# A top-2 mixture of experts in units of two tiles, with weights stationary in the first product and rows added to the output by indirect DMA

## The chip, the cores and the metric

The kernel runs as one program on one core of one Trainium2 chip. The metric is the device time of one execution in microseconds. Three runs of the kernel before took 2163.88, 2171.52 and 2172.83 us; the median is 2171.52 us. The engines are TensorE (PE, its weight loads PEld), VectorE (DVE), ScalarE (ACT), GpSimd (POOL) and SyncE (SP); PEq, SPq and so on are their instruction queues.

## The reference

A batch of 4 images of 256 channels by 32 x 32 positions goes through a Mamba block, a dense product, a channel attention and at last a mixture of experts. Only the last is touched. It sees 4096 tokens of 256 floats, 8 experts and the best 2 experts for each token:

```python
B, S, D = (8, 1024, 256)
E, K, H = (8, 2, 1024)
...
gate_logits = x_flat @ gate_w.T
topk_vals, topk_idx = jax.lax.top_k(gate_logits, K)
topk_w = jax.nn.softmax(topk_vals, axis=-1)
comb = comb.at[jnp.arange(T)[:, None], topk_idx].add(topk_w)
for e in range(E):
    h = jax.nn.gelu(x_flat @ w1[e].T + b1[e], approximate=False)
    y = h @ w2[e].T + b2[e]
    out = out + comb[:, e:e + 1] * y
...
t = t + _L1_ffn_ref(_ln_t(t), L1_ffn_gate_w, ...)
```

All products are in 32-bit floats.

## The kernel before

`build_front` computes everything ahead of the experts. It leaves the normalised tokens in DRAM (`xm_rows`, one row of 1 KB a token), the residual in `x3_dram`, the gate logits in SBUF, and all expert weights in SBUF (`W1`, `W2` inside `experts_sb`). `build_moe` is the stage in question.

**Routing.** VectorE finds the two best experts of each token, TensorE counts tokens by expert with two products, and VectorE turns counts into places. Each expert's list is padded to whole tiles of 128 rows, so that there are always `NT` = 71 tiles. Each step of `step(...)` waits for the one before. Eight rounds of one-hot matrices (L1780 to L1790), multiplied on TensorE, then give for every tile the token of each of its rows (`TAB`, the row to fetch) and the row of `y_rows` to write (`ROW`). `TE` holds the expert of every tile.

**The expert loop, one tile at a time.** Every engine walks the 71 tiles in the order in which its program is written; semaphores tie them together. For a tile t:

- GpSimd gathers 128 rows of `xm_rows` into `XG` by indirect DMA (`gather`, L1562 to L1568, four buffers). It copies the column of indices into `IX` first. It then scatters finished rows: `scatter`, L1570 to L1577, writes `YS` to `y_rows` by indirect DMA. In the loop the gather of tile t stands ahead of the scatter of tile t - 6 (L1592 to L1596).
- TensorE turns the two halves of the rows (`turn_rows`, L1622), multiplies by the expert's first weights (`up`, L1630: the rows stationary, 512 hidden columns moving, 4 products), turns the 8 blocks of the hidden rows (`turn_hidden`, L1639), and multiplies by the second weights (`down`, L1647: 8 products with 256 columns moving). A product of 32-bit floats is two matmul records in the profile, a turn is one. Its `step` (L1662) runs `turn_hidden(t - 1)`, `turn_rows(t + 1)`, `up(t)`, `down(t - 1)`.
- VectorE copies the turned rows (`rows_turned`, L1808) and the hidden rows (`hidden`, L1812) from PSUM, and adds the second bias (`result`, L1816). ScalarE applies the gelu with the first bias from the turned hidden rows (L1693).

**The last part.** When all scatters have landed, SP loads both rows of every token from `y_rows` (L1553) and the last quarter of the residual (L1554). ScalarE and VectorE scale the two rows by their gates and add them to the residual (L1708, L1851, L1855), and SP writes `out` (L1557).

All products of `build_moe` are issued by the helper `mm`, so they all have line 1606 in the profile; their operands tell them apart: `XGT_sb` is `up`, `hgt_sb` with `experts_sb` is `down`, line 1643 is `turn_hidden`, line 1627 is `turn_rows`.

## Time and profile before

| | |
|---|---|
| median of three runs | 2171.52 us |
| profiled execution, its own time | 2172.07 us |
| span of its trace | 2170.1 us |
| mean granted TensorE clock | 0.909 |
| TensorE busy, whole span | 1652.3 us |
| VectorE busy | 1435.5 us |
| GpSimd busy | 1146.9 us |
| ScalarE busy | 868.3 us |
| first `up` of the expert loop starts | 1546.27 us |
| last `down` ends | 2123.78 us |

The shares of the whole span mix stages with different limits. Up to about 1490 us the program is `build_front`, which the change leaves alone apart from where the residual is stored. From there to 1539 us it is the routing, to 2124 us the expert loop, and to the end the last part. A granted clock of 1.00 is 2.4 GHz, 0.50 is 1.2 GHz. Starts are counted from the start of the span.

### The profile page before, as it was taken

The page shows a single profiled execution, that of the slowest core. Times are in us where ns is not written, and L with a number is a line of the kernel's source. Part 1 is how long each engine was busy: PE and PEld are TensorE (multiplying, and loading weights), DVE is VectorE, ACT ScalarE, POOL GpSimd, SP SyncE. Part 2 cuts the span into 40 slices and gives each one's busy share as a digit, 9 for nine tenths or more (in the row PEclk, how much of TensorE's full clock was granted, in tenths as well). Part 3 has the DMA queues.
Part 4 walks back from the last instruction along what each step waited for, and adds up shares of the span by engine and source line. Part 5 has one row for each costly group of instructions (what it writes and reads, how often), then busy time and mean ns, then how long its engine had stood idle before and what let it go on. Part 6 is the DMA issues. An engine that isn't in the chain of part 4 may idle for free. (4 is left out here: it accounts for less than half of the span.)

```text
span 2170.1 us, 22230 instructions
## 1 busy us (share of the span) xinstructions
PE 1652.3 (76%) x5692; PEld 922.6 (43%) x5693; DVE 1435.5 (66%) x1492; ACT 868.3 (40%) x1535; POOL 1146.9 (53%) x708
## 2 busy tenths in 40 slices
PE   5357777677778766777778777664699999999990
PEld 2122234342224443222445222344377667666770
DVE  3989996679997858999577999845422222222224
ACT  6535425464432664543456443221122332233223
POOL 2699872569894438988155989500222332233210
PEclk9789998889999888999877999976799999999995
DMA  3075530055561016654004656443011100110107
GB/s 113 6 250 215 202 127 22 5 177 205 194 223 58 5 30 246 208 198 156 23 5 159 212 194 205 185 191 118 24 32 34 34 31 31 34 34 31 31 23 256
DMA packets 76307, 245.72 MB, mean 113 GB/s; under 512 B 10364, under 2 KB 24197, under 8 KB 71366
## 3 DMA queue, kind: packets, MB, share of 16 engines
q1 hardware_dynamic: 69414, 226.17, 29.9%
q0 software_dynamic: 6816, 18.62, 2.7%
q8 instruction: 37, 0.61, 0.1%
q14 instruction: 40, 0.33, 0.0%
HBM read 220.76 MB, written 23.99 MB: 113 GB/s over the span
## 5 line engine op out<-in xcount | busy, mean ns | idle before, releaser
L368 PE MATMUL psum<-HC_sb,ident_sb 128*128 128x512 f32 x1024 | 492.0, 604 | 59.5 <-DVE HC_sb L1320 57.9
L368 PE MATMUL psum<-experts_sb 64*128 64x512 f32 (+4 forms) x962 | 348.3, 572 | 235.9 <-DVE HC_sb L1320 148.1
L913 ACT ACTIVATE psum<-experts_sb 128x1024 f32<-128x1024 f32 x256 | 285.2, 1117 | 476.0 <-DVE experts_sb L1310 387.9
L1310 DVE TENSOR_TENSOR_SCAN experts_sb<-psum,DBX_sb 128x1024 f32<-128x1024 f32 x172 | 390.0, 2277 | 29.6 <-POOL DBX_sb L1017 28.6
L368 PEld LDWEIGHTS psum<-experts_sb 64*128 64x128 f32 (+4 forms) x962 | 116.6, 168 | 495.4 <-DVE HC_sb L1320 242.9
L368 PEld LDWEIGHTS psum<-HC_sb,ident_sb 128*128 128x128 f32 x1024 | 191.1, 192 | 272.7 <-issue 131.5
L1693 ACT ACTIVATE hgt_sb<-psum_moe,b_sb 128x128 f32<-128x128 f32 x568 | 154.3, 382 | 359.3 <-PE psum_moe L1643 359.1
L1606 PE MATMUL psum_moe<-experts_sb,hgt_sb 128*128 x1136 | 259.4, 382 | 4.1 <-ACT hgt_sb L1693 2.6
L1576 POOL DMA_INDIRECT y_rows<-YS_sb,iy_sb x71 | 70.8, 998 | 356.6 <-PE psum_moe L1627 221.7
L1606 PE MATMUL psum_moe<-experts_sb,XGT_sb 128*128 x568 | 257.0, 595 | 0.3 <-issue 0.3
L1606 PEld LDWEIGHTS psum_moe<-experts_sb,hgt_sb 128*128 128x128 f32 x1136 | 216.3, 191 | 66.8 <-issue 40.6
L1320 DVE TENSOR_TENSOR HC_sb<-psum,experts_sb 128x1024 f32<-128x1024 f32 x192 | 230.7, 1201 | 0.1
L1814 DVE COPY hg_sb<-psum_moe 128x1024 f32<-128x1024 f32 x71 | 87.0, 1225 | 216.5 <-PE psum_moe L1606 216.5
L1017 POOL TENSOR_TENSOR DBX_sb<-DA_sb,experts_sb 128x1024 f32<-128x1024 f32 x88 | 206.1, 2352 | 11.4 <-DVE experts_sb L1310 9.6
L1310 DVE TENSOR_TENSOR_SCAN experts_sb<-psum,SQ_sb 128x1024 f32<-128x1024 f32 x84 | 191.2, 2277 | 0.0
L1025 POOL TENSOR_TENSOR HC_sb<-X_XT_sb,experts_sb 128x1024 f32<-128x1024 f32 x64 | 150.5, 2351 | 76.1 <-PE psum L368 76.0
L1822 DVE TENSOR_TENSOR YS_sb<-psum_moe,b_sb 128x256 f32<-128x256 f32 x71 | 30.2, 425 | 180.8 <-PE psum_moe L1606 180.8
L1606 PEld LDWEIGHTS psum_moe<-experts_sb,XGT_sb 128*128 128x128 f32 x568 | 102.9, 191 | 103.4 <-issue 103.4
L962 POOL TENSOR_TENSOR experts_sb<-experts_sb 128x1024 f32<-128x1024 f32 x16 | 40.4, 2525 | 130.5 <-DVE experts_sb L1095 130.5
L1017 POOL TENSOR_TENSOR DBX_sb<-SQ_sb,experts_sb 128x1024 f32<-128x1024 f32 x44 | 103.5, 2352 | 0.0
L1567 POOL DMA_INDIRECT XG_sb<-xm_rows,ix_sb x71 | 70.4, 991 | 58.1 <-POOL ix_sb L1564 58.1
L950 POOL TENSOR_TENSOR experts_sb<-experts_sb 64x1024 f32<-64x1024 f32 x16 | 37.9, 2369 | 111.1 <-ACT experts_sb L752 109.7
(248 smaller groups left out, 2179.2 us busy)
## 6 DMA issues: line engine op xcount, KB each, us to landing
DA_sb<-b_rows SPq DMA_DIRECT2D x128, 512.0 KB, 4.8
experts_sb<-b_rows SPq DMA_DIRECT2D x64, 512.0 KB, 3.6
SQ_sb<-b_rows SPq DMA_DIRECT2D x64, 512.0 KB, 4.7
X_XT_sb<-c_rows SPq DMA_DIRECT2D x64, 512.0 KB, 5.5
experts_sb<-w1T SPq DMA_DIRECT2D x8, 1024.0 KB, 19.3
experts_sb<-w2T SPq DMA_DIRECT2D x8, 1024.0 KB, 21.3
experts_sb<-y_rows SPq DMA_DIRECT2D x8, 1024.0 KB, 11.8
X_sb<-x_tok SPq DMA_DIRECT2D x5, 1024.0 KB, 6.9
```

Of the source, the lines that this page charges most:

```text
L368: return nc.tensor.matmul(o, lhsT, rhs, start=start, stop=stop, **k)
L913: nc.scalar.activation(decays[i % 2], DT[:, c, :], ACT.Exp, scale=a_neg[:, s:s + 1]).then_inc(da_ready, 1)
L962: nc.gpsimd.tensor_tensor(DT[:, c, :], DTX[:, c, :], log_tile(c), ALU.add).then_inc(dt_done, 1)
L1017: nc.gpsimd.tensor_tensor(DRIVE[i % STATE_SLOTS], B_REP[k], DTX[:, c, :], ALU.mult).then_inc(drive_ready, 1)
L1025: nc.gpsimd.tensor_tensor(HC[:, i % 2, :], C_REP[q % 2], STATE[i % STATE_SLOTS], ALU.mult).then_inc(pool_read, 1)
L1310: v.tensor_tensor_scan(STATE[i % STATE_SLOTS], decays[i % 2], DRIVE[i % STATE_SLOTS], 0.0, ALU.mult, ALU.add).then_inc(h_ready, 1)
L1320: v.tensor_tensor(halves(HC[:, i % 2, :]), crep, halves(STATE[i % STATE_SLOTS]), ALU.mult).then_inc(dve_read, 1)
L1567: pool.indirect_dma_start(XG[:, k, :], None, xm_rows, bass.IndirectOffsetOnAxis(ap=IX[:, k:k + 1], axis=0)).then_inc(xg_ready[k], 16)
L1576: pool.indirect_dma_start(y_rows, bass.IndirectOffsetOnAxis(ap=IY[:, k:k + 1], axis=0), YS[:, k, :], None).then_inc(y_stored[k], 16)
L1606: return nc.tensor.matmul(o, lhsT, rhs, start=start, stop=stop, **k)
L1693: m = nc.scalar.activation(HGT[:, j, :], psum[:, 2 + j // 4, (j % 4) * P:(j % 4 + 1) * P], ACT.Gelu, bias=b1[:, bass.ds(e, 1), j])
L1814: v.tensor_copy(HG[:, :].rearrange("p (h n) -> p h n", h=NH), psum[:, 0:2, :]).then_inc(hg_done, 1)
```

## The change

- Tiles are taken in units. The first 32 units hold two tiles of one expert, the last 7 hold one tile, 39 units for the same 71 tiles. An expert's even tiles go to the paired units, an odd one to a single unit; the routing computes places for both.
- In `up` the first weights are stationary, in blocks of 128 x 128, and the turned rows of the unit move (256 columns, 128 for a single unit): 16 products a unit. The hidden rows come out turned already. `turn_hidden` and the copy `hidden` are gone; ScalarE reads the product itself. For this, VectorE copies the expert's first weights from `experts_sb` to one of two buffers `W1S` for every unit (`copy_weights`, 128 x 2048 floats).
- Each result row is scaled by its gate in `result` by a second VectorE instruction. The gates are turned on TensorE, written to DRAM (`gate_rows`), and gathered for every tile by an indirect DMA of 128 single floats (`gather_gate`).
- `build_front` stores the residual into `out` itself. The rows are added there by an indirect DMA that adds (`scatter_add`). Each of these waits until the one before has landed (semaphore `added`). `y_rows`, `x3_dram` and the whole last part are gone.
- GpSimd's indirect DMAs read their indices from the tables, without the copies to `IX` and `IY`, and its program is written out without a loop. TensorE's `step` is `turn_rows(u + 1)`, `up(u)`, `down(u - 1)`.

The diff, cut to its core; removed functions stand above:

```diff
-RING = 4
-TAIL = RING * (NT // RING - 1) + 1
-Y_ROWS = 3 * TOK + NT * P
-R_DIF, R_CHOSEN, R_ALL = 14, 15, 42
+PAIRS = 32
+UNITS = PAIRS + NT - 2 * PAIRS
+OUT_ROWS = TOK + 2 * P
+R_DIF, R_CHOSEN, R_ALL = 14, 15, 56
...
-                sp.dma_start(x3_dram[b], X2[:, :, :]).then_inc(stored, 16)
+                sp.dma_start(out[0:TOK, :].rearrange("(b n p) c -> b p n c", n=NB, p=P)[b], X2[:, :, :]).then_inc(stored, 16)
...
+        HGT = sb("hgt", [P, 2, HB, 2 * P])
+        W1S = sb("w1s", [P, 2, CT, HID])
+        XG = sb("XG", [P, 4, C])
+        XGT = sb("XGT", [P, 2, CT, 2 * P])
+        YS = sb("YS", [P, 4, C])
...
+            sp.wait_ge(gates_copied, 1)
+            sp.dma_start(gate_rows.rearrange("(a p) o -> a (p o)", p=P), P21T[:, :]).then_inc(gates_stored, 16)
+            sp.wait_ge(gates_stored, 16)
+            sp.wait_ge(added, NT * 16)
...
+            def gather(tile):
+                k = slots(tile)
+                if tile >= 4:
+                    pool.wait_ge(t1_ready, (tile // 2 if tile < 2 * PAIRS else tile - PAIRS) - 1)
+                pool.indirect_dma_start(XG[:, k, :], None, xm_rows,
+                                        bass.IndirectOffsetOnAxis(ap=TAB[:, tile:tile + 1], axis=0)).then_inc(xg_ready[k], 16)
+
+            def gather_gate(tile):
+                pool.indirect_dma_start(PS[:, tile:tile + 1], None, gate_rows,
+                                        bass.IndirectOffsetOnAxis(ap=GIX[:, tile:tile + 1], axis=0)).then_inc(
+                                            gate_there[slots(tile)], 16)
+
+            def scatter_add(tile):
+                pool.wait_ge(y_done, tile + 1)
+                if tile:
+                    pool.wait_ge(added, tile * 16)
+                pool.indirect_dma_start(out, bass.IndirectOffsetOnAxis(ap=SCAT[:, tile:tile + 1], axis=0),
+                                        YS[:, tile % 4, :], None, compute_op=ALU.add).then_inc(added, 16)
 
             pool.wait_ge(tab_done, 1)
+            for tile in range(4):
+                gather(tile)
+            pool.wait_ge(tab_done, 2)
+            pool.wait_ge(gates_stored, 16)
+            for tile in range(4):
+                gather_gate(tile)
+            for u in range(UNITS):
+                if u + 2 < UNITS:
+                    for j in range(width(u + 2)):
+                        gather(first_tile(u + 2) + j)
+                    for j in range(width(u + 2)):
+                        gather_gate(first_tile(u + 2) + j)
+                for j in range(width(u)):
+                    scatter_add(first_tile(u) + j)
...
+            def turn_rows(u, k, ready):
+                for j in range(width(u)):
+                    pe.wait_ge(xg_ready[2 * k + j], ready)
+                if not isinstance(u, int) or u >= 2:
+                    pe.wait_ge(xgt_done, u - 1)
+                for j in range(width(u)):
+                    for c in range(CT):
+                        m = nc.tensor.transpose(psum[:, 6 + k, c * 2 * P + j * P:c * 2 * P + (j + 1) * P],
+                                                XG[:, 2 * k + j, c * P:(c + 1) * P], ident[:, :])
                 m.then_inc(t1_ready, 1)
 
+            def up(u, k):
+                w = width(u) * P
+                pe.wait_ge(w1_copied, u + 1)
+                pe.wait_ge(xgt_done, u + 1)
                 for h in range(NH):
+                    if not isinstance(u, int) or u:
+                        pe.wait_ge(gelu_done, u * 2 + (h - 1))
+                    for q in range(4):
+                        for c in range(CT):
+                            m = mm(psum[:, 2 * h + q // 2, (q % 2) * 2 * P:(q % 2) * 2 * P + w],
+                                   W1S[:, k, c, (4 * h + q) * P:(4 * h + q + 1) * P], XGT[:, k, c, 0:w],
+                                   c == 0, c == CT - 1)
+                    m.then_inc(m1_ready, 1)
...
+            def down(u, k):
+                e = pe.value_load(TE[0:1, bass.ds(u, 1)], min_val=0, max_val=E - 1)
+                if not isinstance(u, int) or u:
+                    pe.wait_ge(y_biased, first_tile(u))
+                pe.wait_ge(gelu_done, u * 2 + 2)
+                for j in range(width(u)):
+                    for q in range(HB):
+                        m = mm(psum[:, 4 + j, 0:C], HGT[:, k, q, j * P:(j + 1) * P], W2[:, bass.ds(e, 1), q, :],
+                               q == 0, q == HB - 1)
+                    m.then_inc(m2_ready, 1)
...
+            def step(u, k, ready):
+                turn_rows(u + 1, (k + 1) % 2, ready)
+                up(u, k)
+                down(u - 1, (k + 1) % 2)
...
+            def gelu(u, k):
+                w = width(u) * P
+                e = act.value_load(TE[0:1, bass.ds(u, 1)], min_val=0, max_val=E - 1)
+                if not isinstance(u, int) or u >= 2:
+                    act.wait_ge(m2_ready, first_tile(u - 1) if isinstance(u, int) else u * 2 - 2)
+                for h in range(NH):
+                    act.wait_ge(m1_ready, u * 2 + (h + 1))
...
+                step(v.tensor_tensor(EQ[:, :, :], POS[:, :, :], by_expert(PAIRF[:, :]), ALU.is_lt))
+                step(v.tensor_tensor(EQ[:, :, :], EQ[:, :, :], by_expert(DELTA[:, :]), ALU.mult))
+                step(v.tensor_tensor(POS[:, :, :], POS[:, :, :], by_expert(SHIFT[:, :]), ALU.add))
+                step(v.tensor_tensor(POS[:, :, :], POS[:, :, :], EQ[:, :, :], ALU.add))
...
+            def copy_weights(u, k):
+                e = dve.value_load(TE[0:1, bass.ds(u, 1)], min_val=0, max_val=E - 1)
+                if not isinstance(u, int) or u >= 2:
+                    dve.wait_ge(m1_ready, u * 2 - 2)
+                v.tensor_copy(W1S[:, k, :, :].unsqueeze(1), W1[:, bass.ds(e, 1), :, :]).then_inc(w1_copied, 1)
+
+            def result(u, j, there, free):
...
+                v.tensor_tensor(ys.unsqueeze(1), psum[:, 4 + j, 0:C].unsqueeze(1), b2[:, bass.ds(e, 1), :],
+                                ALU.add).then_inc(y_biased, 1)
+                dve.wait_ge(gate_there[there[1]], there[2])
+                dve.wait_ge(y_biased, tile + 1)
+                v.tensor_scalar(ys, ys, PS[:, bass.ds(tile, 1)], None, ALU.mult).then_inc(y_done, 1)
```

**GpSimd, before**, one turn of the loop over tiles. L1567 is the gather of tile t, L1576 the scatter of tile t - 6; `t1_ready` is raised by `turn_rows`, `y_copied` by `result`:

```order
L1564 ISA [waits t1_ready]
L1564 COPY ix_sb<-tab_sb 128x1
L1565 REGISTER_ALU
L1567 DMA XG_sb<-xm_rows,ix_sb 128x256 [waits ix_ready]
L1595 ISA
L1572 ISA [waits y_stored0]
L1572 COPY iy_sb<-row_sb 128x1
L1573 REGISTER_ALU
L1576 DMA y_rows<-YS_sb,iy_sb 21376x256 [waits iy_ready,y_copied]
```

**GpSimd, changed**, from the start of the stage through the passes u = 0 and u = 1 of its loop over units. L1561 is a gather of rows, L1565 one of gates, L1573 an adding scatter; `y_done` is raised by the scaling in `result`:

```order
L1561 DMA XG_sb<-xm_rows,tab_sb 128x256 [waits tab_done]
L1561 DMA XG_sb<-xm_rows,tab_sb 128x256 x3
L1565 DMA ps_sb<-gate_rows,gix_sb 128x1 [waits gates_stored,tab_done]
L1565 DMA ps_sb<-gate_rows,gix_sb 128x1 x3
L1561 DMA XG_sb<-xm_rows,tab_sb 128x256 [waits t1_ready] x2
L1565 DMA ps_sb<-gate_rows,gix_sb 128x1 x2
L1573 DMA out<-YS_sb,scat_sb 4352x256 [waits y_done]
L1573 DMA out<-YS_sb,scat_sb 4352x256 [waits added,y_done]
L1561 DMA XG_sb<-xm_rows,tab_sb 128x256 [waits t1_ready] x2
L1565 DMA ps_sb<-gate_rows,gix_sb 128x1 x2
L1573 DMA out<-YS_sb,scat_sb 4352x256 [waits added,y_done] x2
```

The gathers of pass u are those of unit u + 2, and they stand behind the scatters of unit u - 1; before, the gather of a tile stood behind the scatter of the tile seven earlier.

**TensorE, before**, one step of the loop over tiles, the eight `down` products shown by the first:

```order
L1643 MATMUL psum_moe<-m_ident_sb,hg_sb 128x128 x8
L1627 MATMUL psum_moe<-m_ident_sb,XG_sb 128x128 x2
L1606 MATMUL psum_moe<-experts_sb,XGT_sb 128x512
L1648 TENSOR_LOAD te_sb
L1606 MATMUL psum_moe<-experts_sb,hgt_sb 128x256
```

**TensorE, changed**, one step of the loop over units:

```order
L1622 MATMUL psum_moe<-m_ident_sb,XG_sb 128x128 [waits xgt_done,xg_ready3,xg_ready2]
L1622 MATMUL psum_moe<-m_ident_sb,XG_sb 128x128 x3
L1632 ISA [waits xgt_done,w1_copied]
L1595 MATMUL psum_moe<-XGT_sb,w1s_sb 128x256 [waits gelu_done]
L1595 MATMUL psum_moe<-XGT_sb,w1s_sb 128x256 x7
L1595 MATMUL psum_moe<-XGT_sb,w1s_sb 128x256 [waits gelu_done]
L1595 MATMUL psum_moe<-XGT_sb,w1s_sb 128x256 x7
L1641 TENSOR_LOAD te_sb
L1644 REGISTER_ALU [waits y_biased]
```

The eight turns of hidden rows are gone; the turns of the next unit's rows, with their wait for both gathers, are now the first thing in a step, ahead of the products of the present unit.

## Rows read from the trace of the kernel before

**Rows 1.** The page, 40 slices of 54.3 us: engines and granted clock.
```profile
PE   5357777677778766777778777664699999999990
PEclk9789998889999888999877999976799999999995
```

**Rows 2.** Busy time by stretch (TensorE, weights, VectorE, ScalarE, GpSimd, clock, DMA).
```profile
1600.00:1700.00 100.00, 99.60 (x427) 69.51 (x427) 25.74 (x38) 29.84 (x103) 29.50 (x49) 1.00 0.10 32
2100.00:2172.00 72.00, 21.21 (x83) 14.96 (x81) 30.51 (x70) 22.05 (x56) 4.52 (x7) 0.66 0.56 197
```

**Rows 3.** Chain of waits: start, us, engine, tile, line, count.
```profile
1729.69 0.87 PE psum_moe L1643 x8
1730.78 6.89 PE psum_moe L1606 x24
...
1746.75 3.43 PE psum_moe L1606 x8
...
2125.14 2.43 DMA y_rows<-YS_sb,iy_sb
```

**Rows 4.** Timeline, entry of the expert stage.
```profile
1503.45 0.17 DVE L1753 TENSOR_SCALAR padi_sb<-padi_sb 128x8 uint32<-128x8 uint32 x1
...
1504.28 0.42 DVE L1757 TENSOR_TENSOR incl_sb<-incl_sb,tot_sb 128x256 f32<-128x256 f32 x1
1504.73 0.42 DVE L1758 TENSOR_TENSOR incl_sb<-incl_sb,start_sb 128x256 f32<-128x256 f32 x1
...
1538.84 0.20 DVE L1800 TENSOR_SCALAR tab_sb<-row_sb 128x71 uint32<-128x71 uint32 x1
...
1540.26 1.16 POOL L1567 DMA_INDIRECT XG_sb<-xm_rows,ix_sb  x1 [0.97 <-POOL ix_sb L1564]
...
1542.46 0.98 POOL L1567 DMA_INDIRECT XG_sb<-xm_rows,ix_sb  x1 [0.84 <-POOL ix_sb L1564]
...
1545.29 0.69 PE L1627 MATMUL psum_moe<-m_ident_sb,XG_sb 128*128 128x128 f32 x2 [1.31 <-DMA XG_sb<-xm_rows,ix_sb]
...
1546.27 5.04 PE L1606 MATMUL psum_moe<-experts_sb,XGT_sb 128*128 x8 [0.28 <-issue]
```

**Rows 5.** Timeline, last tile and what follows it.
```profile
2118.38 5.40 PE L1606 MATMUL psum_moe<-experts_sb,hgt_sb 128*128 x16 [2.57 <-ACT hgt_sb L1693]
2123.93 0.42 DVE L1822 TENSOR_TENSOR YS_sb<-psum_moe,b_sb 128x256 f32<-128x256 f32 x1 [8.42 <-PE psum_moe L1606]
2125.14 0.99 POOL L1576 DMA_INDIRECT y_rows<-YS_sb,iy_sb  x1 [7.66 <-DVE YS_sb L1822]
```

**Rows 6.** Timeline of two tiles: start, length, engine, line, operation, [idle <-releaser].
```profile
1710.12 3.21 PEld L1606 LDWEIGHTS psum_moe<-experts_sb,hgt_sb 128*128 128x128 f32 x15 [0.24 <-issue]
...
1713.57 1.04 PE L1643 MATMUL psum_moe<-m_ident_sb,hg_sb 128*128 128x128 f32 x8
1713.89 0.43 DVE L1822 TENSOR_TENSOR YS_sb<-psum_moe,b_sb 128x256 f32<-128x256 f32 x1 [2.35 <-PE psum_moe L1606]
...
1714.66 3.60 PE L1606 MATMUL psum_moe<-experts_sb,XGT_sb 128*128 x8
```

**Rows 7.** DMA issues: queue, operation, count, KB each, median us to landing.
```profile
xm_rows<-X_XT_sb SPq DMA_DIRECT2D x4, 1024.0 KB, 4.7
```

**Rows 8.** Gathers of line 1567: who waited (us, times), and time to landing.
```profile
  PE psum_moe L1627: 6.4, 2
...
DMA to landing us min/median/max: 2.6/2.8/3.7
```

**Rows 9.** Busy time by stretch around the last down product.
```profile
2115.00:2118.30 3.30, 0.81 (x8) 0.57 (x6) 0.42 (x1) 2.17 (x8) 1.18 (x2) 1.00 0.11 40
2118.30:2120.30 2.00, 1.92 (x6) 1.61 (x7) 0.00 (x0) 0.00 (x0) 0.00 (x0) 0.68 0.00 0
2120.30:2122.30 2.00, 2.00 (x6) 1.55 (x6) 0.00 (x0) 0.00 (x0) 0.00 (x0) 0.50 0.00 0
2122.30:2124.00 1.70, 1.48 (x7) 0.97 (x5) 0.07 (x1) 0.00 (x0) 0.00 (x0) 0.96 0.00 0
```

More of the change, by code:

```diff
@@ L1468, in lay_out, with build_moe @@
     return a
-def build_moe(nc, t, x3_dram, xm_rows, y_rows, logits, routing, experts, out):
+def build_moe(nc, t, xm_rows, gate_rows, logits, routing, experts, out):
     with ExitStack() as ctx:
@@ new lines, in build_moe @@
+        tab_step = sem("tab_step"); tab_done = sem("tab_done")
+        gates_turned = sem("gates_turned"); gates_copied = sem("gates_copied"); gates_stored = sem("gates_stored")
+        xg_ready = [sem(f"xg_ready{k}") for k in range(4)]; gate_there = [sem(f"gate_there{k}") for k in range(4)]
+        t1_ready = sem("t1_ready"); xgt_done = sem("xgt_done"); w1_copied = sem("w1_copied"); m1_ready = sem("m1_ready"); gelu_done = sem("gelu_done")
+        m2_ready = sem("m2_ready"); y_biased = sem("y_biased"); y_done = sem("y_done"); added = sem("added")
@@ L1540, in build_moe, with width, first_tile, slots @@
         C_ALL = 16 * len(consts)
+        def width(u):
+            return 2 if not isinstance(u, int) or u < PAIRS else 1
+        def first_tile(u):
+            return 2 * u if not isinstance(u, int) or u < PAIRS else u + PAIRS
+        def slots(tile):
+            return tile % 4 if tile < 2 * PAIRS else 2 * ((tile - PAIRS) % 2)
+        def uses(tile):
+            return sum(slots(i) == slots(tile) for i in range(tile + 1))
         @block.sync
@@ L1620, in _ @@
                 i.then_inc(onehot_used, 1)
[L1622 to L1627 removed]
+                if g == 0:
+                    pe.wait_ge(route, R_ALL)
+                    pe.wait_ge(c_loaded, C_ALL)
+                    nc.tensor.transpose(psum[0:2 * NG_, 3, 0:P], P21[:, :, :].rearrange("p j n -> p (j n)"),
+                                        ident[:, :]).then_inc(gates_turned, 1)
@@ L1824, in _ @@
             dve.wait_ge(c_loaded, C_ALL)
+            copy_weights(0, 0)
             rows_turned(0, 0)
+            copy_weights(1, 1)
             rows_turned(1, 1)
-            hidden(0)
-            for k in range(RING):
-                rows_turned(k + 2, k % 2)
-                hidden(k + 1)
-                result(k, k % 2, 16 if k >= 2 else None)
-            with dve.Fori(1, NT // RING - 1) as i:
-                for k in range(RING):
-                    rows_turned(i * RING + (k + 2), k % 2)
-                    hidden(i * RING + (k + 1))
-                    result(i * RING + k, k % 2, i * 32 + (k // 2) * 16)
@@ new lines, in _ @@
+            copy_weights(2, 0)
+            for j in range(2):
+                result(0, j, (j, j, 16), None)
+            rows_turned(3, 1)
+            copy_weights(3, 1)
+            for j in range(2):
+                result(1, j, (2 + j, 2 + j, 16), None)
+            with dve.Fori(1, PAIRS // 2 - 1) as i:
+                for k in range(2):
+                    rows_turned(i * 2 + (k + 2), k)
+                    copy_weights(i * 2 + (k + 2), k)
+                    for j in range(2):
+                        result(i * 2 + k, j, (2 * k + j, 2 * k + j, i * 16 + 16), i * 64 + (32 * k + 16 * j - 48))
@@ L1858 @@
+            for u in range(PAIRS - 2, UNITS):
+                if u + 2 < UNITS:
+                    rows_turned(u + 2, u % 2)
+                    copy_weights(u + 2, u % 2)
+                for j in range(width(u)):
+                    tile = first_tile(u) + j
+                    result(u, j, (tile % 4, slots(tile), 16 * uses(tile)), 16 * (tile - 3))
 def kernel(**inputs):
```

297 lines of the change are left out of this document (98 added, 199 removed).

## The prediction

> **What bounds the kernel now.** I read the 40 slices first: TensorE's row turns from sevens into nines, and its clock into tens, three quarters of the way [rows 1]. That is the expert loop. The busy times by stretch then give it as 99.60 of 100 us of TensorE at a granted clock of 1.00, with VectorE, ScalarE and GpSimd under a third, and the end of the program as something else, 21 of 72 us [rows 2]. The chain of waits shows the loop's beat: 6.89 us of products, 0.87 us of turned hidden rows (L1643), again and again, with no other engine in it [rows 3]. From 1729.69 to 1730.78 and on, a tile takes 0.87 + 0.22 (row turns) + 6.89 = 7.98 us; 71 tiles are 566.6 us of the 577.5 us from the first `up` at 1546.27 [rows 4] to the last `down`'s end at 2118.38 + 5.40 = 2123.78 [rows 5]. So in the loop everything that leaves TensorE is won, and only while TensorE is still never kept waiting. Behind the loop stand 2170.1 - 2123.78 = 46.3 us in which TensorE has nothing to do.
>
> My sum is made against the profiled execution's own 2172.07 us, 0.55 us above the median of the runs, so it needs no correction.
>
> **What is taken off TensorE.** `turn_hidden` is 8 turns a tile, 0.87 us in the chain [rows 3]: 7.98 becomes 7.11 us a tile. `up` in its new form is 16 products, 32 records, of 256 columns with new weights each. That form stands in the trace as `down`: 15 weight loads go by in 3.21 us, 0.214 us each [rows 6]. So a unit of two takes 32 x 0.214 = 6.85 us, against 2 x 3.43 = 6.86 us now [rows 3]: nothing won or lost. In the 7 single units 32 records with 128 columns go at the beat of the turns, 0.87 / 8 = 0.109 us: 3.49 against 3.43 us, 0.4 us in all. If those weight loads didn't overlap, they would cost up to 0.19 us each, 0.08 us x 32 x 7 = 18 us more; I take none, since the turns in the trace load weights at the same beat.
> From first `up` to last `down` TensorE then needs 71 x 7.11 - 0.88 (two units' row turns, now ahead of it) + 0.4 = 504.3 us, and 1.6 us for a start at the low clock, as now (5.04 against 3.43 us, [rows 3, 4]): 505.9 against 577.5 us, -71.6 us. In this are 62 us of turns; the other 10 are waits of the first and the last tile that the new order doesn't have, such as 2.57 us for the last gelu [rows 5].
>
> **The end.** From the last `down` on: 0.16 us to the bias, 0.42 us for it [rows 5], 0.04 us to the next instruction, 0.30 us for the scaling (between 0.2 and 0.43, what a 128 x 256 VectorE instruction takes), 0.79 us until GpSimd starts (2123.93 + 0.42 to 2125.14), about 3.1 us until the added rows have landed (the plain scatter took 2.43 us, [rows 3]), 0.2 us to the end: 5.0 against 46.3 us, -41.3 us.
>
> **The routing** gets 11 steps more of 8 elements at 0.17 + 0.04 = 0.21 us [rows 4], two more of 256 elements net (two fall away, four come) at 0.46 us, one more of 0.2 us and the copy of the turned gates, 0.3 us: 2.3 + 0.9 + 0.5 = +3.7 us. All of it is in VectorE's chain, on which the first gather waits. Then `up(0)` waits for four gathers where it waited for two. The first is issued 0.8 us after the table (now 0.97 behind a copy), four take 1.16 + 0.99 x 2 + gaps of 0.4 between starts, and the last lands 2.83 us after its start (1542.46 to 1545.29, [rows 4]). That is 8.0 + 0.9 us after the table against 1546.27 - 1539.04 = 7.2 us now, +1.6 us. Nothing waits for the gates: they are first used when `down(0)` is over. The residual stored in rows of 1 KB has the shape of the `xm_rows` store, which lands in 4.7 us on a queue that nobody waits for then [rows 7]: 0.
>
> So far 2172.07 - 71.6 - 41.3 + 5.3 = **2064.5 us**, if TensorE never waits inside the loop.
>
> **The wait that comes in.** It does wait. GpSimd's pass u issues the gathers of unit u + 2, then two of gates, then the scatters of unit u, and the pass before ended with the scatters of unit u - 1. These need `down(u - 1)`, the last thing in TensorE's step u. The first thing in step u + 1 is `turn_rows(u + 2)`, which needs those gathers. They are issued only when the step is over, and behind `turn_rows(u + 2)` stand `up(u + 1)` and `down(u)`, whose inputs have long been there. Before, six tiles lay between: TensorE waited for a gather twice [rows 8], both times at the entry. The length of the wait, from the last `down` of a step to the first turn of the next:
> - 0.32 us to the bias on VectorE (1713.57, TensorE free, to 1713.89), 0.42 us for it [rows 6], 0.04 and 0.30 us for the scaling;
> - 0.80 us until GpSimd starts the scatter [rows 5], 0.99 us for it [rows 5], 0.98 us for the first gather [rows 4]; then the second starts, and lands 2.83 us later (2.6 to 3.7, [rows 8]);
> - two gaps between indirect DMAs that follow each other. In the trace each stands behind a copy and 0.84 us of idle time [rows 4], so 0 to 0.84 us; I take 0.40, since part of the 0.84 is the way of the copy's semaphore.
> That is 0.32 + 0.42 + 0.34 + 0.80 + 0.99 + 0.40 + 0.98 + 0.40 + 2.83 = 7.5 us. To it comes what an adding scatter costs over a plain one, which no row shows. It cannot be cheaper in either part, since it moves the same rows and reads the target too. Its issue may take 0.99 to 2.0 us. The second scatter waits until the first has landed; `down`'s halves are 3.46 us apart, so landing later than 3.46 - 0.80 = 2.66 us after its start costs, and the plain one needs 2.43 us, twice as much 4.9 us: 0 to 2.2 us. Of both together (0 to 3.2) I take 0.7, near the plain row. **8.2 us** a wait. A single unit has one gather and no scatter just before its own: 8.2 - 1.39 - 0.35 = 6.45 us.
>
> **The clock comes on top.** After 2.57 us without work ahead of the last `down`, the granted clock stood at 1.00, then 0.68, 0.50, and 0.96 over the next 5.7 us (0.50 is the 1.2 GHz level), and the 16 records took 5.40 us [rows 5, 9]. At 0.214 us each they are 3.43 us, with the overhang of the last one's end 3.6 us. I take 5.40 - 3.6 = 1.8 us for each wait. Bounds: 0, if the clock stays up, and 2.5.
>
> Waits occur ahead of units 3 to 38, that is 29 double ones and 7 single ones (units 0 to 2 are gathered ahead of the first scatter): 29 x (8.2 + 1.8) + 7 x (6.45 + 1.8) = 290 + 57.8 = 347.8 us. **2064.5 + 347.8 = 2412 us**, 11% slower. With the shortest terms (6.3 and 5.3 us, no clock loss) 220 us and 2284 us; with the longest (12.8 and 8.6 us, 2.5 us of clock) 521 us and 2586 us.
>
> The copy of the weights (128 x 2048 floats; the trace has 1024 from PSUM in 1.23 us, so about 2.5 us at most) follows `rows_turned` on VectorE, and is used a step later, 14 us on: 0. Nothing else waits behind it but `result`, 7 us later.
>
> **Rivals.**
> 1. *The add is dear.* On the same rows: issue 2.0 and landing 4.9 us, so the wait is 7.5 + 1.0 + 2.2 = 10.7 us (single 7.1): 29 x 12.5 + 7 x 8.9 = 425 us, **2489 us**. For it: the target must be read before it can be written. Against: 128 KB are little for 16 DMA engines, used 10% in this stage [rows 2]. The Trainium skill, Collectives: The Full Stack, section on why ReduceScatter is half of AllGather, says that an add in the DMA path costs because it needs two source reads and two descriptors a chunk, not for the arithmetic. By that rule this rival is the forecast; no run yet shows it for a scatter.
> 2. *The clock stays up.* 36 x 1.8 = 65 us less: **2347 us**. Against: the one gap of 2.57 us [rows 5, 9] already brought the low level.
> 3. *The gathers are there in time: faster.* The place is the same wait at `turn_rows`. If GpSimd's chain from `down` to landed rows costs TensorE less than (2172 - 2064.5) / 36 = 3.0 us a unit, clock included, the time falls below the present one; at none it is **2064 us**. For it: before, the chain never reached TensorE. Against: the landing alone takes 2.6 us at the least [rows 8] and two issues 2.0 us, and the order of the program leaves no way round.
> 4. *The new `up` does not keep its beat*, with every weight load of 0.19 us bared in 1024 + 224 records: 237 us more, **2649 us**. Against: `down` has the same form and keeps it [rows 6]. It is among the others below.
>
> The Trainium skill, DMA: Bandwidth & Descriptors, section on the anatomy of a DMA on the GpSimd path, gives about 2.0 us plus the bytes over 436 GB/s, an estimate of 2.3 us for these 128 KB, where the gathers here take 2.8 us from start to landing. By it the wait would be 0.5 us shorter, 18 us over the loop; the trace's figure is used.
>
> **Chances.** Forecast (2350 to 2460) 0.6; dear add 0.2; clock stays up 0.1; in time or nearly 0.05; other 0.05. Differences under 0.5% I count as no change. Faster 0.05, same 0.01, slower 0.94. The range 2320 to 2510 holds the forecast, most of rival 1 and of rival 2.
>
> **What would show it.** In the new profile TensorE's `turn_rows` should have idle time of about 8 us a unit ended by the DMA into `XG`, 36 times, and its share in the loop should be near 65% at a granted clock of 0.8 to 0.9. The chain of waits should run `down`, bias, scaling, scatter, gathers, landing, turns, products. Records of `up` 0.214 us apart after the clock is back, and under 6 us from the last `down` to the end, would confirm the other terms. The forecast is wrong if TensorE is 95% busy in the loop, or if the wait stands at another semaphore (`w1_copied`, `y_biased`, `gelu_done`).

## The result and the profile after

The changed kernel takes 2469.78 us (median of 4 runs, 2463.57 to 2470.72), the kernel before 2167.70 us in the same comparison: a ratio of 1.1386, with a 95% interval from 1.1349 to 1.1424. It is 14% slower; 2412 us had been forecast, with a range of 2320 to 2510. The span of the profiled execution is 2468.9 us, its mean granted clock 0.854.

The page of the kernel after, 40 slices of 61.7 us, against [rows 1]:

```profile
PE   5277776777778777777677673667575666757665
PEclk9699988899987899988899885878788787877877
```

The nines of the expert loop have become fives to sevens, and the clock's nines sevens and eights. Busy time by stretch (columns as in [rows 2]):

```profile
1600.00:1700.00 100.00, 65.93 (x268) 56.33 (x269) 13.38 (x23) 12.55 (x32) 27.58 (x24) 0.80 0.12 20
...
2400.00:2469.00 69.00, 41.21 (x214) 37.76 (x214) 8.84 (x16) 9.26 (x32) 12.97 (x11) 0.75 0.12 17
```

TensorE is busy 66 of 100 us, where it was 99.6, at a granted clock of 0.80; in the last stretch no combining of rows is left. The chain of waits through one wait of TensorE (start, us, engine, tile and line), which answers to the two-term beat of [rows 3]:

```profile
1800.28 0.44 DVE YS_sb L1840
...
1800.91 0.36 DVE YS_sb L1844
...
1801.55 3.91 DMA out<-YS_sb,scat_sb
...
1805.49 0.75 issue
1806.24 1.57 POOL out L1573
1807.81 0.30 issue
1808.11 1.02 POOL XG_sb L1561
1809.13 0.30 issue
1809.44 2.83 DMA XG_sb<-xm_rows,tab_sb
1812.27 0.23 issue
1812.51 1.11 PE psum_moe L1622 x4
1813.62 12.69 PE psum_moe L1595 x48
```

From the top: the bias (L1840) and the scaling (L1844) of the first half's rows, the adding scatter of them, 3.91 us from its start to its landing, 0.75 us until GpSimd is off again, the second scatter, the two gathers, and 2.83 + 0.23 us until the second one's rows can be turned. No gap in it belongs to TensorE. TensorE's own timeline around it (start, length, [idle before <-releaser]):

```profile
1796.43 7.07 PE L1595 MATMUL psum_moe<-experts_sb,hgt_sb 128*128 x32
1812.51 1.11 PE L1622 MATMUL psum_moe<-m_ident_sb,XG_sb 128*128 128x128 f32 x4 [9.01 <-DMA XG_sb<-xm_rows,tab_sb]
1813.41 9.43 PE L1595 MATMUL psum_moe<-XGT_sb,w1s_sb 128*128 128x256 f32 x32
...
1839.43 8.38 PE L1595 MATMUL psum_moe<-XGT_sb,w1s_sb 128*128 128x256 f32 x32
```

It stood still for 9.01 us. Then 32 records of the first product took 9.43 us, though the same count of `down` just before had taken 7.07. In the next unit they took 8.38 us; the two values alternate through the loop of double units. The granted clock (last but two of the columns) in stretches of that wait says why:

```profile
1804.00:1808.00 4.00, 0.00 (x0) 0.00 (x0) 0.43 (x2) 0.00 (x0) 1.57 (x1) 0.99 0.18 27
1808.00:1812.50 4.50, 0.00 (x0) 0.00 (x1) 0.00 (x0) 0.00 (x0) 3.47 (x4) 0.50 0.48 87
...
1816.00:1818.00 2.00, 2.00 (x6) 1.62 (x5) 0.00 (x0) 0.00 (x0) 0.00 (x0) 0.50 0.00 0
1818.00:1822.00 4.00, 4.00 (x19) 3.47 (x19) 0.00 (x0) 1.57 (x4) 0.00 (x0) 0.98 0.00 0
```

In the last 4.5 us of the wait, and still while the first product ran, it was 0.50, the 1.2 GHz level; it came back after 1818. The waits by sum, count and longest:

```profile
PE psum_moe L1622 <- DMA XG_sb<-xm_rows,tab_sb: 182.0, 23, 9.2
PE psum_moe L1622 <- issue: 133.9, 15, 9.6
```

These 38 waits hold the two at the entry (6.0 and 1.4 us). The other 36 sum to 315.9 - 7.4 = 308.5 us, 29 ahead of double units, 8.90 us on average, and 7 ahead of single ones, 7.20 us on average (6.1 to 8.3). In some the releaser is put down as "issue", but their lengths and their place are the same. GpSimd's DMAs (count, median us from start to landing):

```profile
XG_sb<-xm_rows,tab_sb POOLq DMA_INDIRECT x71, 2.8
ps_sb<-gate_rows,gix_sb POOLq DMA_INDIRECT x71, 2.3
out<-YS_sb,scat_sb POOLq DMA_INDIRECT x71, 3.8
```

The adding scatter lands after 3.8 us, the plain one took 2.43 [rows 3]. The end, against [rows 5]:

```profile
2455.17 3.71 PE L1595 MATMUL psum_moe<-experts_sb,hgt_sb 128*128 x16 [0.73 <-DVE YS_sb L1840]
2459.04 0.42 DVE L1840 TENSOR_TENSOR YS_sb<-psum_moe,b_sb 128x256 f32<-128x256 f32 x1 [3.56 <-PE psum_moe L1595]
...
2460.23 1.56 POOL L1573 DMA_INDIRECT out<-YS_sb,scat_sb  x1 [2.90 <-DVE YS_sb L1844]
```

From the last `down`'s end at 2455.17 + 3.71 = 2458.88 to the end of the span are 10.0 us, against 46.3. The entry, against [rows 4]: the first gather starts 0.49 us after the last step of the table (1541.84, 0.20 us long) has begun, and the first `up` 4.4 us later than in the kernel before.

```profile
1542.33 1.16 POOL L1561 DMA_INDIRECT XG_sb<-xm_rows,tab_sb  x1 [108.03 <-DMA gate_rows<-p21t_sb]
...
1550.64 9.40 PE L1595 MATMUL psum_moe<-XGT_sb,w1s_sb 128*128 128x256 f32 x32
```

### The profile page after: what moved, and what is told of

Its sections match the earlier page's. It is cut to its first block and busy times, and to the rows that moved or that the text cites. A ratio compares the mean times of both kernels' runs of the same rounds, so it can differ in the third digit from the quotient of the medians.

```text
span 2468.9 us, 20712 instructions
## 1 busy us (share of the span) xinstructions
PE 1679.8 (68%) x5805; PEld 1039.2 (42%) x5806; DVE 1393.2 (56%) x1451; ACT 806.2 (33%) x1240; POOL 1229.8 (50%) x637
## 5 line engine op out<-in xcount | busy, mean ns | idle before, releaser
L1573 POOL DMA_INDIRECT out<-YS_sb,scat_sb x71 | 113.4, 1597 | 623.9 <-DVE YS_sb L1844 526.6
L1688 ACT ACTIVATE hgt_sb<-psum_moe,b_sb 128x256 f32<-128x256 f32 (+1 forms) x312 | 116.6, 456 | 777.7 <-PE psum_moe L1595 777.6
L1595 PE MATMUL psum_moe<-XGT_sb,w1s_sb 128*128 128x256 f32 (+1 forms) x1248 | 324.3, 432 | 0.0
L1595 PEld LDWEIGHTS psum_moe<-XGT_sb,w1s_sb 128*128 128x128 f32 x1248 | 276.7, 243 | 41.5
L1840 DVE TENSOR_TENSOR YS_sb<-psum_moe,b_sb 128x256 f32<-128x256 f32 x71 | 30.1, 424 | 446.7 <-PE psum_moe L1595 446.7
L1622 PE MATMUL psum_moe<-m_ident_sb,XG_sb 128*128 128x128 f32 x142 | 39.5, 428 | 315.9 <-DMA XG_sb<-xm_rows,tab_sb 182.0
L1595 PE MATMUL psum_moe<-experts_sb,hgt_sb 128*128 x1136 | 251.7, 379 | 0.7 <-DVE YS_sb L1840 0.7
L1825 DVE COPY XGT_sb<-psum_moe 128x512 f32<-128x512 f32 (+1 forms) x39 | 25.1, 644 | 317.3 <-PE psum_moe L1622 317.3
L1622 PEld LDWEIGHTS psum_moe<-m_ident_sb,XG_sb 128*128 128x128 f32 x142 | 24.7, 213 | 330.5 <-issue 277.2
L1561 POOL DMA_INDIRECT XG_sb<-xm_rows,tab_sb x71 | 71.2, 1003 | 129.4 <-DMA gate_rows<-p21t_sb 108.0
```

The costliest lines, as they stand in the source:

```text
L1561: pool.indirect_dma_start(XG[:, k, :], None, xm_rows, bass.IndirectOffsetOnAxis(ap=TAB[:, tile:tile + 1], axis=0)).then_inc(xg_ready[k], 16)
L1573: pool.indirect_dma_start(out, bass.IndirectOffsetOnAxis(ap=SCAT[:, tile:tile + 1], axis=0), YS[:, tile % 4, :], None, compute_op=ALU.add) ...
L1595: return nc.tensor.matmul(o, lhsT, rhs, start=start, stop=stop, **k)
L1622: m = nc.tensor.transpose(psum[:, 6 + k, c * 2 * P + j * P:c * 2 * P + (j + 1) * P], XG[:, 2 * k + j, c * P:(c + 1) * P], ident[:, :])
L1688: m = nc.scalar.activation(HGT[:, k, 4 * h + q, 0:w], psum[:, 2 * h + q // 2, (q % 2) * 2 * P:(q % 2) * 2 * P + w], ACT.Gelu, bias=b1[:, b ...
L1840: v.tensor_tensor(ys.unsqueeze(1), psum[:, 4 + j, 0:C].unsqueeze(1), b2[:, bass.ds(e, 1), :], ALU.add).then_inc(y_biased, 1)
```

## The experiments

The theory was that one thing makes the time: a unit's gathers stand behind scatters that need the end of the step just over, so that TensorE waits at the head of the next step, and its clock falls. The rivals: the adding scatters are the cost in themselves; GpSimd's pass is too long; the new products are slow. `e1` to `e8` are edits of the changed kernel, `e9` and `e10` of the kernel before.

**Gathers a pass ahead (e1).**

```diff
-                for j in range(width(u)):
-                    scatter_add(first_tile(u) + j)
+                if u:
+                    for j in range(width(u - 1)):
+                        scatter_add(first_tile(u - 1) + j)
+            for j in range(width(UNITS - 1)):
+                scatter_add(first_tile(UNITS - 1) + j)
```

> The changed kernel with GpSimd's scatters one pass later: pass u issues the gathers of unit u + 2 and then the scatters of unit u - 1, so that a gather no longer stands behind a scatter of the step just over. Theory (place in the order): the wait of 9.2 us ahead of each unit's row turns and the low clock behind it (2.9 us more) go, 29 x 12.1 + 7 x 9 = 414 us: about 2060 us, TensorE over 98% busy in the loop, granted clock 1.00. Rival (the adding scatters are too slow in themselves): GpSimd has 2 scatters 4.7 us apart, 2 gathers and 2 gate gathers, 11.7 us of 14.2 us a unit; if the adds slow the gathers or pile up, the loop stays bound by GpSimd and the time stays above 2150 us, with TensorE waiting for gathers or for the scatters' semaphore.

Measured: 2073.08 us (2070.34 to 2073.25), ratio to the kernel before 0.9545 (0.9529 to 0.9561). 397 us of the changed kernel's time go with the place of 71 scatters. The expected 2060 us was 13 us too low: it priced every wait by the one in the timeline above (9.2 us, and 2.9 us for the clock), where the averages are 8.9 and 2.45 us. Busy time, and the timeline of a step:

```profile
1600.00:1700.00 100.00, 100.00 (x479) 88.06 (x478) 23.94 (x42) 21.93 (x56) 52.83 (x42) 1.00 0.22 37
```

```profile
1802.88 0.60 PE L1625 MATMUL psum_moe<-m_ident_sb,XG_sb 128*128 128x128 f32 x4
...
1803.32 7.07 PE L1598 MATMUL psum_moe<-XGT_sb,w1s_sb 128*128 128x256 f32 x32
...
1808.80 1.02 POOL L1561 DMA_INDIRECT XG_sb<-xm_rows,tab_sb  x1 [0.30 <-issue]
...
1810.23 7.07 PE L1598 MATMUL psum_moe<-experts_sb,hgt_sb 128*128 x32
```

In this stretch TensorE is never idle and the clock is full. A unit takes 14.25 us (1802.88 to 1817.13 for the next one's turns). The gathers (1808.80) now run beside the first product. Theory confirmed, and both rivals about GpSimd and the adds fall: all the same scatters and gathers are in this kernel. The products keep their beat: 32 records of `up` and 32 of `down` take 6.91 us from start to start each.

**Plain scatter, and plain scatter without the chain (e2, e3).**

```diff
...
-                pool.indirect_dma_start(out, ..., YS[:, tile % 4, :], None, compute_op=ALU.add).then_inc(added, 16)
+                pool.indirect_dma_start(y_rows, ..., YS[:, tile % 4, :], None).then_inc(added, 16)
...
```
```diff
...
-                if tile:
-                    pool.wait_ge(added, tile * 16)
...
-                                        YS[:, tile % 4, :], None).then_inc(added, 16)
+                                        YS[:, tile % 4, :], None).then_inc(added[tile % 4], 16)
...
```

Nothing is added to the output, so these kernels don't compute the reference. The target is now `y_rows`, so the row numbers differ too, and the routing has one step less to compute them.

> The changed kernel with its order kept, but the scatter writes into rows of its own instead of adding (the additions to the output are left out); each scatter still waits for the one before. Theory: the adding costs 0.6 us of issue (1.60 to 1.0) and 1.3 us because the first scatter of a unit lands after 3.8 us and not 2.45; the wait falls from 9.2 to 7.3 us: 29 x 1.9 + 7 x 0.6 = 59 us, about 2411 us. Rival (the adds also slow the gathers behind them on the same queue): the landing of the gathers falls from 2.8 us too and the time is below 2390 us.

> As the run before, and scatters no longer wait for each other (one semaphore for each of the four result buffers; additions left out). Theory: a plain scatter lands before the second one's rows are ready (2.45 against 3.46 - 0.3 us), so the chain of waits costs nothing here: within 5 us of the run before, about 2411 us. Rival (the wait for the scatter before is a cost of its own, whatever lands): 10 us or more below it.

Measured: 2408.42 and 2407.21 us (two runs each). GpSimd's scatter in e2 by its median landing, and its issue and the row turns in the timeline:

```profile
y_rows<-YS_sb,scat_sb POOLq DMA_INDIRECT x71, 2.4
```

```profile
1812.66 0.99 POOL L1573 DMA_INDIRECT y_rows<-YS_sb,scat_sb  x1 [2.45 <-DVE YS_sb L1843]
...
1818.04 1.08 PE L1622 MATMUL psum_moe<-m_ident_sb,XG_sb 128*128 128x128 f32 x4 [6.88 <-issue]
```

Adding to `out` rather than writing to `y_rows` costs 61 us in all: landing 3.8 against 2.4 us, issue 1.6 against 0.99 us, and the wait ahead of a double unit falls from 8.9 to 7.0 us on average. What the other rows and the step less have to do with it isn't separated. The gathers land after 2.8 us in both, so the adds don't slow them. With plain scatters the chain of semaphores costs nothing that these runs can tell (the two of e3 lie 8.6 us apart). With adds it does: in the chain above the second half's rows were ready at 1804.29 + 0.35 = 1804.64, and its scatter started at 1806.24. Of these 1.6 us some 0.3 are its ordinary start; 1.3 are the landing of the first add (3.91 us) and the 0.78 us until GpSimd was off again, as far as they exceed the distance between the halves.

**Busy while waiting (e4).**

```diff
+                if not isinstance(u, int) or u >= 2:
+                    pe.wait_ge(xgt_done, u - 1)
+                if not isinstance(u, int) or u >= 3:
+                    for _ in range(64 if width(u) == 2 else 48):
+                        nc.tensor.transpose(psum[:, 6 + k, 0:P], ident[:, :], ident[:, :])
                 for j in range(width(u)):
                     pe.wait_ge(xg_ready[2 * k + j], ready)
-                if not isinstance(u, int) or u >= 2:
-                    pe.wait_ge(xgt_done, u - 1)
```

> The changed kernel with its order kept; ahead of each wait for the gathers TensorE does 64 turns of the identity (48 for a single unit) into the PSUM bank that the row turns will overwrite, 7.0 and 5.2 us of work that nobody uses. The wait for the rows stays as it is; only the clock can change. Theory: the low clock behind the wait costs 2.9 us a unit (first product 9.3 instead of 6.85 us, row turns at 0.9 instead of 0.44): 29 x 2.9 + 7 x 2.6 = 102 us less, about 2368 us. Rival (the products are slow for another reason, such as their operands' buffers): the first product stays at 9.3 us and the time at 2470 us or above.

Measured: 2389.10 us (2387.45 to 2393.91), 81 us below the changed kernel where 102 had been expected. TensorE's timeline of one wait, and busy time by stretch:

```profile
1807.65 7.15 PE L1620 MATMUL psum_moe<-m_ident_sb 128*128 128x128 f32 x64
1816.62 0.63 PE L1625 MATMUL psum_moe<-m_ident_sb,XG_sb 128*128 128x128 f32 x4 [1.83 <-DMA XG_sb<-xm_rows,tab_sb]
1817.09 7.07 PE L1595 MATMUL psum_moe<-XGT_sb,w1s_sb 128*128 128x256 f32 x32
```

```profile
1600.00:1700.00 100.00, 90.89 (x572) 82.94 (x571) 14.59 (x25) 12.53 (x32) 33.03 (x29) 1.00 0.15 25
```

From the end of `down` to the row turns it is 8.97 us as before, 7.15 us of it useless turns. With the clock at 1.00 the products behind it take 7.07 instead of 9.43 us. Between the starts of two units' row turns lie 23.4 us on average of 27 units, 25.6 in the changed kernel: the clock costs 2.2 us a double unit. Of the cause only that part is the clock; the wait itself stays.

**Row turns between the products (e5).**

```diff
             def step(u, k, ready):
-                turn_rows(u + 1, (k + 1) % 2, ready)
                 up(u, k)
+                turn_rows(u + 1, (k + 1) % 2, ready)
                 down(u - 1, (k + 1) % 2)
...
```

> The changed kernel with GpSimd's order kept, and TensorE's row turns moved from the head of a step to between the first and the second product. The wait for the gathers then starts 6.91 us later (3.5 us in a single unit). Theory (only the place of the wait counts): it falls from 8.87 to 1.96 us a double unit and from 7.06 to 3.6 us a single one. If a wait of 2 us leaves the clock up: 2470 - 29 x (6.91 + 2.2) - 7 x 3.5 = 2181 us; if it falls all the same, 29 x 2.2 more: 2245 us. Rival (GpSimd's pass is the bound): the wait doesn't shrink by what TensorE does ahead of it, and the time stays above 2300 us.

Measured: 2191.58 us (2182.34 to 2195.81), between the two values of the theory, and 0.9% above the kernel before (0.6 to 1.1). A row of the turns, and busy time:

```profile
1820.93 0.63 PE L1622 MATMUL psum_moe<-m_ident_sb,XG_sb 128*128 128x128 f32 x4 [1.85 <-issue]
```

```profile
1600.00:1700.00 100.00, 88.06 (x401) 74.62 (x399) 19.59 (x35) 17.86 (x46) 41.17 (x35) 0.98 0.19 31
```

The wait is 1.85 us, near the 2.0 of 8.90 - 6.91. The clock mostly stays up (0.98). A double unit takes 17.2 us on average: 14.25, 1.9 for the wait, 0.4 that TensorE now waits between the turns and `down`, and 0.65 that are left for the clock. These stem from some units only: most take 16.8 to 17.1 us, a few 18 and more, as the one ahead of the row above, in which the 32 records of `down` (at 1803.81) took 8.37 us instead of 7.1. GpSimd's pass, unchanged, is not the bound.

**Gathers between the two scatters (e6).**

```diff
...
             for u in range(UNITS):
-                if u + 2 < UNITS:
...
-                for j in range(width(u)):
-                    scatter_add(first_tile(u) + j)
+                n = range(width(u + 3)) if u + 3 < UNITS else ()
+                scatter_add(first_tile(u))
+                for j in n:
+                    gather(first_tile(u + 3) + j)
+                if width(u) == 2:
+                    scatter_add(first_tile(u) + 1)
+                for j in n:
+                    gather_gate(first_tile(u + 3) + j)
```

The gathers for unit 2 are issued ahead of this loop.

> The changed kernel with the gathers of a unit issued between the two adding scatters that they stood behind (for single units the order is as it was). They no longer wait for the second half of the second product, nor for the landing of the first add. From the end of a step: 0.32 + 0.98 us for the first half's rows, 3.46 us earlier, then 0.3 + 1.6 us of scatter, 0.3 + 1.02 + 0.3 us and 3.07 us to landed rows: a wait of 4.4 us instead of 8.87. Theory (the chain's terms add up as read): 29 x 4.45 = 129 us less with the same loss by the clock, about 2341 us. If the shorter wait loses less of it, down to 2280 us. Rival (the rows' landing is held by the adds in flight on the same queue): the gathers now overlap the first add and land later than 3.1 us after their start, and the gain is under 80 us.

Measured: 2300.49 us (2297.02 to 2304.43), 169 us less. One wait in the timeline:

```profile
1817.61 1.62 POOL L1573 DMA_INDIRECT out<-YS_sb,scat_sb  x1 [11.03 <-DVE YS_sb L1849]
1819.53 0.99 POOL L1561 DMA_INDIRECT XG_sb<-xm_rows,tab_sb  x1 [0.30 <-issue]
...
1820.82 0.95 POOL L1561 DMA_INDIRECT XG_sb<-xm_rows,tab_sb  x1 [0.30 <-issue]
...
1823.58 1.09 PE L1627 MATMUL psum_moe<-m_ident_sb,XG_sb 128*128 128x128 f32 x4 [4.03 <-issue]
```

The wait is 4.2 us on average ahead of the double units. I had reckoned 4.4 from the terms, and the second gather, started 3.2 us after an add that is then still in flight, lands in its usual time (1820.82 to 1823.58; the median of all gathers of rows is 2.8 us as before): the rival falls. Only the gathers of gates, which nobody waits for here, now land after 2.7 instead of 2.3 us; they stand right behind the second add and in part beside the copy of the weights, and no run separates the two. The double units' period is 20.5 us, 5.1 less than in the changed kernel; 28 of them are 143 us, and the waits ahead of the first three single units fall from 7.3 to 8.3 us to 2.5 to 3.6 us too. The expected 2341 us forgot those. The clock's part is 20.5 - 14.25 - 4.2 = 2.1 us, against 25.6 - 14.25 - 8.9 = 2.5 us in the changed kernel: half the wait saves little of it.

**Gathers ahead with plain scatters, and with the turns in the middle (e7, e8).** The edits are those of e1 and e2, and of e1 and e5.

> The version with the gathers a pass ahead, with plain scatters into rows of their own (the additions to the output are left out). Theory: where nothing waits for the scatters, adding costs nothing; only the end gets shorter, by the 1.3 us of an add's landing and 0.6 us of issue: 2070 to 2073 us against 2073 us. Rival (the adds slow TensorE or VectorE in the loop): 10 us or more below.

> Both orders changed: gathers a pass ahead and row turns between the products. In the version with the gathers ahead TensorE waits 0.3 us once in the loop, so there is next to nothing left to win: 2070 to 2075 us. Rival: the turned rows are now copied by VectorE right before the results, and the results come later, 0.7 us at the last units: up to 2078 us.

Measured: 2067.34 us (2064.83 to 2069.64) and 2071.28 us (2067.52 to 2072.56; ratio 0.9539, 0.9521 to 0.9558). e7 is 5.7 us below e1, more than expected and less than the rival's 10. In its trace the first `up` starts 3.8 us earlier (1547.49 against 1551.30), which is ahead of every scatter, and from there to the end of the last `down` it is 508.8 against 510.0 us. An add that nobody waits for costs next to nothing in the loop. The end did not behave as expected. The last `down` of e7:

```profile
2052.55 3.72 PE L1598 MATMUL psum_moe<-experts_sb,hgt_sb 128*128 x16 [0.73 <-DVE YS_sb L1842]
```

From 2052.55 + 3.72 = 2056.27 to the end of its span at 2067.8 are 11.5 us, where e1 has 9.9: with a plain scatter the end is 1.6 us longer, though that scatter is issued and landed sooner. In e2 it is 11.6 us too. e8 can't be told from e1.

**The order alone, in the kernel before (e9, e10).**

```diff
...
-            with pool.Fori(2, NT // RING) as i:
+            with pool.Fori(1, NT // RING) as i:
                 for k in range(RING):
                     gather_next(i, k)
-                    pool.wait_ge(y_stored[k % 2], i * 32 + ((k - 6) // 2) * 16)
-                    scatter(i * RING + (k - 6), k % 2)
+                    pool.wait_ge(y_stored[k % 2], i * 32 + ((k - 2) // 2) * 16)
+                    scatter(i * RING + (k - 2), k % 2)
...
```

The start and the end of GpSimd's program are fitted to it: the first two scatters now stand ahead of the loop. e10 is edited in the same way, with k - 3.

> The kernel before with nothing changed but GpSimd's order: the gather of tile t + 1 stands behind the scatter of tile t - 2 instead of t - 6, so that it is issued only when the step ahead of the one that needs it is over. Units, stationary weights and adding scatters are not in it. Theory (the order alone makes the wait): from the end of a step 0.32 + 0.42 us for the rows, 0.8 + 1.0 us of scatter, 0.2 + 0.8 us of copy and issue, 2.83 us to landed rows = 6.4 us, less 0.87 us of turned hidden rows at the head of the step: a wait of 5.5 us and 2.2 us by the clock for each of 67 tiles, 515 us: about 2685 us. Rival (the wait comes from the adding scatters, the gate gathers or the units): within 1% of 2171 us.

> As the run before, but the gather of tile t + 1 stands behind the scatter of tile t - 3, one more step ahead. Theory: the chain of 6.4 us now lies beside a step of 7.98 us: no wait, 2168 to 2176 us. Rival (each pass of GpSimd is too long for a short lead): TensorE waits in every step, over 2200 us.

Measured: 2778.22 us (ratio 1.2804, 1.2757 to 1.2852) and 2172.91 us (1.0005, 0.9994 to 1.0017). One wait of e9, and a stretch of e10:

```profile
1807.75 0.43 DVE L1819 TENSOR_TENSOR YS_sb<-psum_moe,b_sb 128x256 f32<-128x256 f32 x1 [2.35 <-PE psum_moe L1603]
1808.97 0.99 POOL L1576 DMA_INDIRECT y_rows<-YS_sb,iy_sb  x1 [13.59 <-DVE YS_sb L1819]
...
1811.01 1.00 POOL L1567 DMA_INDIRECT XG_sb<-xm_rows,ix_sb  x1 [0.84 <-POOL ix_sb L1564]
...
1813.89 0.68 PE L1624 MATMUL psum_moe<-m_ident_sb,XG_sb 128*128 128x128 f32 x2 [5.42 <-DMA XG_sb<-xm_rows,ix_sb]
```

```profile
1600.00:1700.00 100.00, 99.56 (x424) 69.77 (x423) 26.12 (x37) 28.71 (x98) 29.25 (x50) 1.00 0.10 33
```

With neither units nor adds, the same step too few of lead makes the kernel before 28% slower, and one tile more gives all of it back. e9's waits are 5.6 us on average (375.6 us in 67, the two at the entry left out), as reckoned. A tile takes 17.1 us on average, so that 17.1 - 8.0 - 5.6 = 3.5 us are left, where 2.2 had been taken for the clock; 67 times that difference is nearly all of the miss of the expected 2685 us. Behind a wait the granted clock is 0.50 from 1797 to 1803, nearly all of the first product, whose 8 records take 6.26 us there (at 1797.88) and took 3.60 in the kernel before [rows 6]. In the changed kernel the first product loses 1.3 or 2.4 us.

## Why the prediction was right

Step by step, the forecast's terms beside what the runs show:

| term | forecast | measured |
|---|---|---|
| entry, first `up` later by | 5.3 us | 5.0 us (e1) |
| first `up` to last `down`, no waits | 505.9 us | 510.0 us (e1) |
| last `down` to the end | 5.0 us | 9.9 us (e1) |
| time without waits in the loop | 2064.5 us | 2073.1 us (e1) |
| wait, double unit | 8.2 us | 8.9 us |
| wait, single unit | 6.45 us | 7.2 us |
| clock, each wait | 1.8 us | 2.45 us |
| all 36 waits with the clock | 347.8 us | 396.7 us |
| time | 2412 us | 2469.8 us |

The measured time lies 10 us above the 2350 to 2460 us that had been given a chance of 0.6, and inside the range, which was drawn wide enough for most of the first rival. Of the 57.5 us that are missing, 25.5 are the waits, 23.4 the clock and 8.6 the time without waits; so across these terms no errors cancelled, and inside the wait they did in part, as told below.

- **What bounds the kernel, and what is taken off TensorE:** right. The turned hidden rows were 0.87 us a tile on the one busy engine; with the waits out of the way a unit takes 14.25 us, against 15.96 for two tiles. The new form of `up` costs what the row of `down` said. Of the 4.1 us by which the loop without waits was too short, 0.7 are the start at the low clock (9.40 - 7.07 = 2.3 us, not 1.6) and 0.73 a wait of the last `down` for the bias; the rest isn't traced.
- **The wait that comes in:** right in place, in number (36) and in cause; e1 removes it by the order alone, e9 makes it by the order alone. In its size two errors met. Some terms were too dear: GpSimd starts 0.29 us after VectorE's semaphore, not 0.80, the gaps between its DMAs are 0.30, not 0.40, and the bias starts 0.15 us after `down`'s end, not 0.32 (the 0.32 was counted from the start of the next record at 1713.57, while the last of `down` ran to 1710.11 + 3.62 = 1713.73). The 0.80 was read rightly, but from an issue that took a copied index; how the change makes it 0.29 no run separates. The add costs more than the 0.7 us taken: the trace has 0.6 us of issue and, in the unit shown, 1.3 us that the second scatter waits for the first one's landing. That is 1.9 us, halfway between the forecast's 0.7 and the first rival's 3.2. Scaling and its wait take 0.56 instead of 0.34 us, and the landing with TensorE's start 3.07 instead of 2.83. Together 25.5 us over the 36 waits. (The longest wait of 12.8 us doesn't come out of the bounds given for its parts, which add up to 12.6.)
- **The clock:** right that it falls each time; 1.8 us was too small. Behind every other wait of a double unit it costs some 2 us, behind those between some 3. I had read it from one case, the last `down` after 2.57 us of idle time, where the clock was still full for the first part of the product [rows 9]. After a wait of 9 us it is low from the first row turn on. 396.7 - 308.5 = 88 us, or 2.45 each; e4 gives 81 us back. The second rival, that the clock stays up, falls for waits of 4 us and more.
- **The end:** the gain is 36.4 us where I had 41.3. The forecast named under 6 us as a sign of being right; it is 10.0, so this sign failed. The last scatter starts at 2460.23, and at the median landing of 3.8 us it would be over at 2464.0, but the span ends at 2468.9. No row shows what fills the 5 us. Adding doesn't make it: with plain scatters (e2, e7) the same stretch is some 8 us. Its cause stays open.
- **The first rival (a dear add)** comes nearest in its time, 2489 us (19 us off, the forecast 58), but only since it had the clock too cheap as well. Of its two prices the landing is 3.8 of the 4.9 us that it asked, the issue 1.6 of 2.0. The Trainium skill, Collectives: The Full Stack, section on why ReduceScatter is half of AllGather, puts an add in the DMA path of a ring collective at twice the reads and descriptors of a copy. For this scatter of 128 rows of 1 KB the runs show 1.6 times the issue and 1.6 times the landing; the direction agrees, the factor is the measured one.
- **The third rival (the gathers are in time)** is what the changed kernel would have been with its scatters one pass later. I gave it 0.05, since the written order excluded it.

The version of e1 (2073 us) and that of e8 (2071 us) beat both kernels, by 4.5% the kernel before. Nothing of the change's arithmetic is slow; only the order of two kinds of DMAs on one queue was.

## What to carry to other kernels

Where one engine's queue both fetches ahead and stores behind, count the steps between a fetch and the store it stands behind: the fetch is issued only when that store's rows exist, however early its buffer is free. Price a short lead as the whole chain (result, store's issue, fetch's issue, landing) plus the clock that TensorE loses behind each wait, and compare it with one step of work. An adding DMA cost next to nothing here while nobody waited for it (e1 against e7), and 61 us where the next scatter and the gathers stood behind it (e2): its longer issue, and its landing as far as the next rows were ready before it.
